# One graph edge step moved ahead of an attention's products, and the query exponentials inside the feed-forward split into units

## The reference, cut to what matters

```python
# graph branch
m = jnp.concatenate([h[edge_src], w], axis=1)
tmp = jax.nn.relu(m @ W1.T + b1)
h_N = jax.ops.segment_sum(tmp, edge_dst, num_segments=h.shape[0])
# transformer branch, 4 layers
q = jax.nn.softmax(split(x @ Wq) * scale, axis=-1)
k = jax.nn.softmax(split(x @ Wk) * scale, axis=-2)
context = jnp.einsum('bhnd,bhne->bhde', k, v)
out = jnp.einsum('bhnd,bhde->bhne', q, context)      # then @ Wo + bo, residual
x = x + (jax.nn.gelu(h @ W1[i] + b1[i], approximate=False) @ W2[i] + b2[i])
x = x + L0_mix + L0_gnn; x = x + experts(layernorm(x))
```

## Time and profile before

| | |
|---|---|
| median of three runs | 2212.54 us (2208.65 to 2212.66) |
| the profiled execution's own time | 2203.06 us |
| its span, first to last instruction | 2201.3 us |
| PE busy | 1919.0 us, 87% |
| DVE busy | 1417.3 us, 64% |
| POOL busy | 1381.6 us, 63% |
| ACT busy | 952.5 us, 43% |
| mean granted TensorE clock | 0.966 |

### The profile page before, as it was taken

How to read it: one execution, slowest core, us unless ns; L and a number is a source line. 1 busy time by engine, 2 the same in 40 slices (tenths; PEclk the granted TensorE clock), 3 DMA queues, 4 the chain that set the end, 5 groups by cost and what they waited for, 6 DMA issues and landing times.

```text
span 2201.3 us, 31538 instructions
## 1 busy us (share of the span) xinstructions
PE 1919.0 (87%) x10094; PEld 1567.0 (71%) x10094; DVE 1417.3 (64%) x3153; ACT 952.5 (43%) x1998; POOL 1381.6 (63%) x1154
## 2 busy tenths in 40 slices
PE   6888999998899999888999988899999894999990
PEld 4666787776677777676877766777777683888880
DVE  8678777767877776677777766876766558211115
ACT  3644444446444443555434446444443321333333
POOL 7767776677586667657766676586667300576650
PEclk9999999999999999999999999999999975999995
DMA  8754333345433333543333345533333421999998
GB/s 198 205 149 114 102 99 73 74 114 158 110 87 95 83 76 82 143 126 97 94 83 72 73 106 156 118 85 85 84 74 92 114 79 52 287 310 299 310 289 182
DMA packets 265013, 287.77 MB, mean 131 GB/s; under 512 B 138881, under 2 KB 195396, under 8 KB 264868
## 3 DMA queue, kind: packets, MB, share of 16 engines
q0 software_dynamic: 127488, 134.76, 25.8%
q1 hardware_dynamic: 133268, 151.21, 22.8%
q10 hardware_dynamic: 4112, 0.03, 0.1%
HBM read 242.07 MB, written 42.72 MB: 129 GB/s over the span
## 4 chain that ended last, share of the span: by engine, by line
PE 53%; DVE 18%; ACT 9%; DMA 8%; issue 6%; POOL 4%; DVEq 1%; SPq 0%; ACTq 0%; POOLq 0%
PE bank L1288 23%; PE bank L1441 10%; POOL G L932 3%; PE bank L446 3%; PE bank L447 3%; PE bank L454 2%; PE bank L1361 2%; PE bank L1553 2%; ACT zr L462 2%; DVE zl L468 2%; DMA TTQ<-zn_d,slot_tok 2%; DVE z L494 2%; DMA y_d<-eT,slot_row 2%; PE bank L1561 2%; PE bank L1376 2%
## 5 line engine op out<-in xcount | busy, mean ns | idle before, releaser
L932 POOL DMA_INDIRECT G<-P_d,src_T x896 | 1134.1, 1266 | 506.8 <-DVE z L494 278.7
L468 DVE SCALAR_TENSOR_TENSOR zl<-z,zr 125x512 fp32r<-125x512 f32 x448 | 289.9, 688 | 145.8 <-ACT zr L462 132.6
L462 ACT ACTIVATE zr<-z 125x512 fp32r<-125x512 f32 x448 | 266.4, 628 | 265.0 <-DVE z L494 218.4
L1441 PE MATMUL bank<-TT,W_s 128*128 128x250 f32 (+1 forms) x1280 | 361.4, 426 | 15.9 <-ACT hid L1147 15.9
L494 DVE TENSOR_TENSOR z<-bank,G 125x512 f32<-125x512 f32 x448 | 289.9, 685 | 115.0 <-PE bank L454 41.2
L1288 PE MATMUL bank<-W_s,hid 128*125 128x256 f32 x1600 | 361.1, 379 | 2.2 <-ACT hid L1147 2.2
L1288 PEld LDWEIGHTS bank<-W_s,hid 128*125 128x125 f32 x1600 | 293.9, 188 | 45.9 <-ACT hid L1147 3.8
L1441 PEld LDWEIGHTS bank<-TT,W_s 128*128 128x128 f32 x1280 | 234.0, 189 | 111.4 <-ACT hid L1147 23.1
L446 PE MATMUL bank<-zr,onehot 125*125 125x256 f32 x896 | 262.2, 326 | 41.0 <-DVE zl L468 39.8
L1147 ACT ACTIVATE hid<-bank,b_s 128x375 f32<-128x375 f32 x320 | 163.2, 521 | 302.2 <-PE bank L1441 286.7
L447 PE MATMUL bank<-zl,onehot 125*125 125x256 f32 x896 | 223.7, 280 | 0.0
(11 more groups left out here) (325 smaller groups left out, 2915.9 us busy)
## 6 DMA issues: line engine op xcount, KB each, us to landing
W_s<-in_L_ffn_w SPq DMA_DIRECT2D x64, 512.0 KB
hid<-in_L_ffn_w SPq DMA_DIRECT2D x64, 512.0 KB
G<-P_d,src_T POOLq DMA_INDIRECT x896
TTQ<-nT_d SPq DMA_DIRECT2D x20, 626.0 KB
W_s<-in_L_mix_W SPq DMA_DIRECT2D x8, 1024.0 KB
nT_d<-TT SPq DMA_DIRECT2D x12, 626.0 KB
aT<-attr_d SPq DMA_DIRECT2D x224, 26.4 KB
nT_d<-TTQ SPq DMA_DIRECT2D x8, 626.0 KB
```

Source lines behind the costliest of these rows:

```text
L462: nc.scalar.activation(zr[:, s, k, :], z[:, k, :], ACT.Relu).then_inc(r_done, 1)
L468: nc.vector.scalar_tensor_tensor(zl[:, k, :], z[:, k, :], 0.0, zr[:, s, k, :].bitcast(f32), ALU.max, ALU.subtract).then_inc(lo_done, 1)
L932: pool.indirect_dma_start(G[:, j, :], None, P_d[:, :], bass.IndirectOffsetOnAxis(ap=src_T[:, at:at + 1], axis=0)).then_inc(g_in[j], 16)
L1441: ins = pe.matmul(to[:, 0:(b - a) * T], W1_s[:, k, part], TT[:, k, TT_PIECES[pc]], start=k == 0, stop=k == KD - 1)
```

## The change

Two edits. On PE and DVE the edge step that stood between unit 1 and unit 2 of the attention stands ahead of all three units, in the four handovers of each layer (16 in all); the attention of group 0, ahead of the feed-forwards, keeps its step in the middle. On ACT, the one exponential over five tiles after f = 5 becomes three: unit 0 after f = 2, unit 1 after f = 4, unit 2 after f = 5, in the 12 feed-forwards with queries inside.

```diff
+        FF_EXP = {2: 0, 4: 1, 5: 2}
...
+                def q_unit(g, i):
+                    a, b = RP[i]
+                    act.wait_ge(row_dve, row_q(l, g) + i + 2)
+                    ins = act.activation(qe[:, a:b, :], qe[:, a:b, :], ACT.Exp, scale=SCALE)
+                    if i == NRP - 1:
+                        ins.then_inc(q_exp, 1)
...
-                        if QIN[g] and f == 5:
-                            q_softmax(g + 1)
+                        if QIN[g] and f in FF_EXP:
+                            q_unit(g + 1, FF_EXP[f])
...
                     if g + 1 < NG:
                         queries_T(g + 1)
-                        attention(g + 1, (0, 1))
                         step(e0 + len(FF_STEPS[g]))
-                        attention(g + 1, (2,))
+                        attention(g + 1, range(NRP))
...
-                def attention(g, middle):
+                def attention(g, ahead=None, middle=None):
                     r = row_ao(l, g)
+                    step(ahead)
                     residual(g, r, 0)
                     residual(g, r, 1)
                     row_stats(g, r, 0, st5b, b_stat)
...
-                        attention(g + 1, e0 + len(FF_STEPS[g]))
+                        attention(g + 1, ahead=e0 + len(FF_STEPS[g]))
```

More of the change, by code:

```diff
@@ L1870, in _ @@
                 step(eM - 1)
-                attention(0, eM)
+                attention(0, middle=eM)
                 queries(1, (0,))
```

## The result

The change takes 2245.04 us (median of six runs, 2241.39 to 2252.04) against 2212.6 for the kernel before (six runs, 2208.65 to 2217.95). The ratio is 1.015, 95% interval 1.0127 to 1.0173: 32.4 us slower, where +29 and 2242 us were forecast.

What follows compares the result with a forecast made beforehand. PE, busy 87% of the span, was taken as the bound, so only time ahead of PE instructions counts. Terms 10.2 + 16.0 - 1.7 + 4.8 gave +29 us, 2242 us on the median; range 2227 to 2253.

Steps and rivals of the forecast that it cites:

- Part 1: Handovers of groups 1 to 3 (12): PE's wait for `QT` becomes one of about 1.3 us for `zl`.
- Part 2: Same 12 handovers: unit 2 waits 0.66 us for DVE's first residual behind the moved step, losing 0.85 us per handover.
- Part 3: Handover to group 1 (4): late gathers hold DVE's step, PE stands 3.8 us, a loss of 4.0 us per handover.
- Part 4: ACT's exponential by units in 12 feed-forwards: added table loads hidden, a gain of 0.14 us in each.
- Part 5: The four pauses of 3.8 us in handovers to group 1 lower TensorE's clock, taken at 1.2 us each.

Runs made afterwards that it cites:

- PE's half alone: Kernel before, with only PE making the step's products ahead of the attention, DVE's order unchanged: 2223.96 us against 2216.09, ratio 1.0035.
- the filled kernel: The kernel of the 4 handovers, with unit 1's attention products made three more times there before use: 2230.5 us, ratio 1.0082 to the kernel before.
- the experiment with DVE's half: Kernel before, with only DVE doing its part of the step before the residuals, PE's order unchanged: 2302.99 us against 2216.09, ratio 1.0392.
- the kernel of the 4 handovers: Kernel before, with the step ahead on PE and DVE in the handover to group 1 alone, exponential whole: 2236.59 us, ratio 1.0095.

## Why the prediction was right, and where it was off

The forecast of +29 us met +32.4, and every step that it named is in the rows. That the sum came so close is in part luck: two terms were too small, and one was too large.

*Part 1, the step on PE.* Right. The wait for `QT` is replaced by one for `zl`, of 1.09 us where 1.3 was worked out. PE's half alone shows that no cover is won even when nothing else is in the way; it is in fact 0.3 us a stretch dearer.

*Part 2, the step on DVE.* Right in its mechanism, 0.27 us short: the moved step with the exponential whole makes a stretch 61.62 us long, 1.12 more than before, where 0.85 was worked out, and the new wait is 0.80 us in place of 0.66. I let DVE's `z` start 0.06 us ahead of the end of the `zl` before it, as like instructions do, and PE 0.05 us behind the residual. In the rows after, the `z` starts 0.04 us behind the `zl` (1254.19 + 1.28, then 1255.51) and PE 0.15 us behind the residual (1258.84 and some 0.68, then 1259.67). That makes 0.2 of it. The half changes show whose wait it is: with DVE's half undone it vanishes, with PE's half undone it grows to 3.1 us.

*Part 3, the handover to group 1.* Right in its mechanism, too large in its sum. The wait is 3.7 to 3.9 us in three layers, but 2.2 in the fourth, where PE came to the step later (it waited 0.26 us for `zl` there, and 1.18 in the others). Counted from the turned queries, unit 2 starts 3.9, 4.1, 3.8 and 1.8 us later than before. With the waited start of its records that is 13.9 us where 16.0 was predicted: I had taken the third layer's 4.0 for all four. The gather, only read from a pair of 1.38 us, stands in DVE's rows by name.

*Part 4, the exponentials.* Right: 0.14 us was predicted, and the stretches show 0.14 with the step at its place (60.36 against 60.50) and 0.16 with it moved (61.46 against 61.62). Both are below what a median can tell. The explanation, that the loads ahead of f = 5 nearly cancel the shorter exponential, was tested by moving them: -0.64 us a stretch.

*Part 5, the clock.* Right that the pauses bring it down, too small in its price. I took 1.2 us for each; the filled kernel shows 1.6 to 1.7 for a fall of 3.4 us, the whole of the 1.69 that the key products cost. In the change, the part from unit 2 to the next turned queries takes 55.7, 56.7, 55.7 and 55.7 us behind the four pauses and 54.0 in the other groups, so 7.7 us in all where 4.8 was predicted. My discount for the share of the low stretch that lies in the pause was wrong in three layers: there the clock fell at the pause's end or after it. Only in the second, where it was down for 6.8 us, did part of that lie in the pause. Nor did I apply the term to the experiment with DVE's half, for which I allowed "some clock loss" and whose pauses of 3.1 us cost 2.2 to 3.0 us each in clock.

*The sum.* Part 2 was short by 12 x 0.27 = 3.2 us and part 5 by 2.9, and part 3 was 2.1 too large. The handovers to group 1 come out at 20.9 us where parts 3, 4 and 5 gave 20.2, but only because two errors cancel. And the prediction's premise that PE has no wait of over 0.3 us until the next f = 7 does not hold in group 4, where two of 1.46 us for `zl` follow. They were the same length after, so nothing was absorbed, as forecast.

## What to carry to other kernels

Work moved into a hole on one engine has a share on the others, and each in-order engine runs that share ahead of what stood there. Ask first what the moved work itself waits for (here the `zl` of the step before, made by the engine that the hole was waiting for), then who is queued behind it on the partner engine, and who waits for that through a shared bank. A short instruction split from a long one paid here only where its table loads fell into idle time that no due time followed closely. And when two kernels' stretches are compared for the price of the clock, begin to count where the pause ends: what lies ahead of it moves for other reasons.

## What the runs showed of the hardware

Each of the 28 pauses of 2.2 to 4.0 us that PE made ahead of unit 2 went with a stretch at the lower clock, which began in the pause or within 1.3 us behind it: 4 in the change, 4 in the kernel with the exponential whole, 4 in the kernel of the 4 handovers and 16 in that with DVE's half alone. Behind the start of unit 2, a low stretch of 3.4 us cost 1.5 to 1.7 us and one of 6.8 us 2.7 to 3.0. Twelve records of repeated products in such a pause kept the clock up and gave the 1.7 us back in all four layers; the medians, 6.1 us apart, agree but do not show it by themselves. The Trainium skill ("TensorE: Matmul & The Clock Gate", What's actually happening) states that an idle PE falls to 1.2 GHz; the trace agrees, with PEclk 0.50 behind the pauses and 1.00 with the fill. Behind pauses of about 1 us the clock mostly stayed, though not always (it fell at five handovers with PE's half alone), and which of them brings it down differs between executions of one kernel. By the price above, six falls more make an estimated 10 us between the two profiled executions.
